# Experts' matrix products cut into four groups of 32 columns, and expert work dealt out step by step instead of in rounds of two steps

## What is computed

```python
# x: 2 batches x 2048 tokens x 256; H = 16 heads of 16; 8 experts, 256 -> 1024 -> 256
qk = (x @ Wqk).reshape(b, n, H, dh).transpose(0, 2, 1, 3)
v  = (x @ Wv ).reshape(b, n, H, dh).transpose(0, 2, 1, 3)
logits = (2.0 * qk @ qk.T - q2[..., :, None] - q2[..., None, :]) / math.sqrt(dh) * tau
out = softmax(logits) @ v                       # for each of 2 x 16 heads, 2048 x 2048
...
top1 = argmax(softmax(x @ router_W + router_b))  # one expert per token
h = relu(x @ W1[e] + b1[e])                      # 256 -> 1024
y = h @ W2[e] + b2[e]                            # 1024 -> 256
out = gate[e] * y
```

## Time and profile before

| what | value |
|---|---|
| median of 3 timed runs | 1456.67 us (1454.11 to 1459.45) |
| profiled execution, its own time | 1452.68 us |
| span of the profiled execution, first to last instruction | 1451.0 us |
| mean granted clock of TensorE | 0.993 of full speed |
| TensorE matmuls, busy | 1383.5 us, 95% |
| ScalarE, busy | 1066.9 us, 74% |
| VectorE, busy | 393.8 us, 27% |
| pairs 3 to 15, with expert work | 296.7 to 1329.0 us of the span |

### The profile page before, as it was taken

One profiled execution on the slowest core, in us unless ns is written; L12 is line 12 of the kernel. 1 busy time (PEld: TensorE's weight loads), 2 busy tenths in 40 slices (PEclk: granted clock), 3 DMA queues, 4 the chain that ended last, 5 costly groups with the idle time before them and its releaser, 6 DMA issues. The chain is left out here.

```text
span 1451.0 us, 26979 instructions
## 1 busy us (share of the span) xinstructions
PE 1383.5 (95%) x9041; PEld 659.9 (45%) x9041; DVE 393.8 (27%) x1009; ACT 1066.9 (74%) x1183; POOL 221.8 (15%) x310
## 2 busy tenths in 40 slices
PE   7999999999999999999999999999999999999978
PEld 5652222234444444444444444444444444445867
DVE  5863000012121211121121212111111212113977
ACT  5669999987777777777777777777777777774122
POOL 3111700001010010000010100100000101001860
PEclk9999999999999999999999999999999999999989
DMA  5779425526446444445464464443454645633423
GB/s 171 267 237 238 143 41 141 131 38 161 122 107 175 107 149 105 106 114 159 106 173 108 106 175 107 146 113 111 113 148 106 175 106 119 184 131 103 141 87 116
DMA packets 125520, 195.47 MB, mean 135 GB/s; under 512 B 22344, under 2 KB 91848, under 8 KB 122024
## 3 DMA queue, kind: packets, MB, share of 16 engines
q1 hardware_dynamic: 116440, 177.22, 44.6%
q0 software_dynamic: 9040, 17.71, 4.4%
HBM read 154.63 MB, written 35.95 MB: 131 GB/s over the span
## 5 line engine op out<-in xcount | busy, mean ns | idle before, releaser
L961 ACT ACTIVATE shared<-ps 128x1024 f32<-128x1024 f32 x1024 | 982.8, 1023 | 242.2 <-PE ps L1100 242.2
L1115 PE MATMUL ps<-shared,work 128*17 128x512 f32 x4096 | 502.5, 600 | 0.5 <-issue 0.5
L1100 PE MATMUL ps<-mov,stat 52*128 52x512 f32 x2048 | 420.6, 466 | 36.1 <-ACT shared L961 31.7
L1100 PEld LDWEIGHTS ps<-mov,stat 52*128 52x128 f32 x2048 | 168.6, 184 | 416.4 <-ACT shared L961 388.1
L1006 DVE TENSOR_SCALAR work<-ps,work 128x128 f32<-128x128 f32 x312 | 109.6, 351 | 590.3 <-PE ps L1167 575.4
L1115 PEld LDWEIGHTS ps<-shared,work 128*17 128x17 f32 x4096 | 89.7, 96 | 217.1 <-issue 203.6
L1167 PE MATMUL ps<-work,XNW 128*128 128x128 f32 x1248 | 180.7, 288 | 0.0
L1167 PEld LDWEIGHTS ps<-work,XNW 128*128 128x128 f32 x1248 | 151.0, 191 | 56.9 <-issue 56.9
L1151 PE MATMUL ps<-XNW,work 128*128 128x256 f32 x624 | 166.2, 382 | 0.0
L799 POOL DMA_DIRECT2D y_slots<-work x39 | 21.9, 563 | 760.1 <-DVE work L998 706.2
L1151 PEld LDWEIGHTS ps<-XNW,work 128*128 128x128 f32 x624 | 104.5, 191 | 11.4 <-issue 4.8
(11 more groups left out here) (168 smaller groups left out, 668.5 us busy)
## 6 DMA issues: line engine op xcount, KB each, us to landing
XNW<-in_L_ffn_W_dram SPq DMA_DIRECT2D x78, 1024.0 KB, 7.1
stat<-q_parts SPq DMA_DIRECT2D x192, 128.0 KB
mov<-q_parts SPq DMA_DIRECT2D x192, 64.0 KB
xg<-in_L_attn_x_dram SPq DMA_DIRECT2D x16, 512.0 KB, 4.7
q_parts<-XNW SPq DMA_DIRECT2D x16, 512.0 KB, 5.4
x_slots<-work SPq DMA_DIRECT2D x1, 4992.0 KB, 16.3
early<-x_slots SPq DMA_DIRECT2D x39, 128.0 KB, 2.1
early<-in_L_ffn_b_dram SPq DMA_DIRECT2D x39, 128.0 KB, 8.3
```

Of the source, the lines that this page charges most:

```text
L961: nc.scalar.activation(probs[:, s % DEEP, half * 1024:(half + 1) * 1024], ps[:, 2 * half:2 * half + 2].rearrange("p a b -> p (a b)"), ACT. ...
L1100: last = nc.tensor.matmul(ps[:, 2 * half + r], stat[rows, hh, m * P:(m + 1) * P], mov[rows, hh, half * 512:(half + 1) * 512], start=True, ...
L1115: last = nc.tensor.matmul(ps[32 * j:32 * j + VW, AV], Vh[:, hh, m], probs[:, s % DEEP, j * 512:(j + 1) * 512], start=(m == 0), stop=(m == ...
```

## The change

Every expert matmul is cut into four, each with 32 columns of weights and with `tile_position=(0, at)`, the form that `values` has. The transposes of `x` become matmuls with the identity in the same form. `expert_plan()` now makes 32 steps in place of 16 rounds: a tile takes 11 steps, `x` in the first, `h` of f in step 1+f, `y` of f in step 2+f. PE issues in each step: logits of the next step, the step's expert units (`y`, `x`, `h` in this order), `values` of this step. VectorE follows the same plan.

```diff
-        ROUNDS = STEPS // 2
+        CW = 32
...
-            rounds = [[] for _ in range(ROUNDS)]
+            steps = [[] for _ in range(STEPS)]
             for tt in range(3):
-                at = 5 * tt
-                rounds[at] += [("x", tt, 0), ("x", tt, 1)]
+                at = 11 * tt
+                steps[at] += [("x", tt, 0), ("x", tt, 1)]
                 for f in range(FC):
-                    rounds[at + 1 + f // 2].append(("h", tt, f))
-                    late = (f + 1) // 2 if tt < 2 else f // 2
-                    rounds[at + 2 + late].append(("y", tt, f))
-            return [sorted(r, key=lambda u: "xhy".index(u[0])) for r in rounds]
+                    steps[at + 1 + f].append(("h", tt, f))
+                    steps[at + 2 + f].append(("y", tt, f))
+            return [sorted(r, key=lambda u: "yxh".index(u[0])) for r in steps]
...
-                        ins = nc.tensor.matmul(ps[:, Y, 0:D], hT[:, b], w2s[:, a, b],
-                                               start=(b == 0), stop=(b == FC - 1))
+                        for at in range(0, P, CW):
+                            ins = nc.tensor.matmul(ps[at:at + CW, Y, 0:D], hT[:, b, at:at + CW], w2s[:, a, b],
+                                                   start=(b == 0), stop=(b == FC - 1), tile_position=(0, at))
...
-                        nc.tensor.transpose(ps[:, bank(k), 0:P], xs[:, a, b * P:(b + 1) * P],
-                                            ident[:, :]).then_inc(ring_ready, 1)
+                        for at in range(0, P, CW):
+                            last = nc.tensor.matmul(ps[at:at + CW, bank(k), 0:P], xs[:, a, b * P + at:b * P + at + CW],
+                                                    ident[:, :], start=True, stop=True, tile_position=(0, at))
+                        last.then_inc(ring_ready, 1)
...
                         for c in range(KC):
-                            last = nc.tensor.matmul(ps[:, bank(k), 0:P], w1s[:, a, c, b * P:(b + 1) * P],
-                                                    xsT[:, a, c], start=(c == 0), stop=(c == KC - 1))
+                            for at in range(0, P, CW):
+                                last = nc.tensor.matmul(ps[at:at + CW, bank(k), 0:P],
+                                                        w1s[:, a, c, b * P + at:b * P + at + CW], xsT[:, a, c],
+                                                        start=(c == 0), stop=(c == KC - 1), tile_position=(0, at))
...
-                    for n in range(ROUNDS):
-                        logits(i, 2 * n + 1)
-                        for u in rounds[n]:
-                            expert(i, u, use)
-                        if n + 1 < ROUNDS:
-                            logits(i, 2 * n + 2)
+                    for s in range(STEPS):
+                        if s + 1 < STEPS:
+                            logits(i, s + 1)
                         elif not last_one:
                             logits(i + 1, 0)
-                        values(i, 2 * n)
-                        values(i, 2 * n + 1)
+                        for u in steps[s]:
+                            expert(i, u, use)
+                        values(i, s)
```

More of the change, by code:

```diff
@@ L983, in expert_body @@
                 def expert_body(i):
-                    rounds = expert_plan()
-                    use = use_numbers(rounds)
-                    for n in range(ROUNDS):
-                        if n == 0:
+                    steps = expert_plan()
+                    use = use_numbers(steps)
+                    for s in range(STEPS):
+                        if s == 0:
                             turn_o(i - 1, 1)
-                        if n == ROUNDS // 2:
+                        if s == TB:
                             turn_o(i, 0)
-                        for u in rounds[n]:
+                        for u in steps[s]:
                             kind, a, b = u
```

## The result

The changed kernel takes 1461.29 us (median of 20 runs, 1455.89 to 1467.60) against 1456.91 us (20 runs) for the kernel before: ratio 1.0032, interval 1.0019 to 1.0044. That is 2.8 to 6.4 us slower. The forecast was slower by 10 us, 1467, with a range of 1430 to 1494. The profiled execution took 1467.6 us, the slowest of the 20, so its other stages have to be kept apart from the change.

What follows compares the result with a forecast made beforehand. PE was taken to bound full rounds, with PE and ACT waiting for each other in light ones. Pairs -22, jumps +24 and clock +8 us gave +10: 1463 profiled, 1467 on the timed runs' scale, range 1430 to 1494.

Steps and rivals of the forecast that it cites:

- The pair without the jump: Pairs 3 to 15: 77.5 us each in place of 79.18, -22 us over 13 pairs (-53 to +7).
- full step: Logits, h, y and values on PE, 21 steps a pair: 2.54 us each, against 5.12/2 = 2.56 before.
- light steps: The 11 steps a pair with x, h or y alone, or empty: 2.2 us taken as their mean.
- The bounds 1.98 and 2.4: Limits for a light step: 1.98 us as in pairs without experts, about 2.4 after a full step, when ACT starts late.
- The sets of four: Four 32-column matmuls side by side in the expert blocks on PE: 0.11 us a set for h, as one matmul before.
- rival 2: Expert sets of four on PE run slower than 0.11 us: +27 us, 1494 with the stall, 1462 without; chance 0.13.
- tail: Sets of four slower still: +187 us if each waits for its own loads, +200 at about 62 ns per matmul.
- The jumps: Ten jumps back of PE's loop over pairs 4 to 14 wait for code: 2.4 us exposed each, +24 us (+11 to +43).
- The 3.3 us: Wait for a code packet at a jump back, chosen nearer the quick 2.0 us transfer than the slow 8.3; bounds 2.0 and 5.2.
- the rest streams in behind its back: After a jump's first packet, later code arrives while PE works, a packet lasting 9 us of work: no further wait.
- The clock: Falls to half clock behind the jumps in every second pair, 1.66 us more each: +8 us (0 to +17).

Runs made afterwards that it cites:

- written-out form: The changed kernel with TensorE's hardware loop over pairs 4 to 14 replaced by eleven copies of its code: 1429.73 us, ratio 0.9816 to the kernel before.
- 1557: The changed kernel, looped, with x, y and the third tile's h back in the old whole form: 1489.86 us in one run against 1456.87 before.
- 2037: The changed kernel with its hardware loop, but the transposes of x back in the old whole form: ratio 1.0387 to the kernel before.
- 1749: The changed kernel with its hardware loop, but x and y back in the old whole form: ratio 1.0445 to the kernel before.
- the form alone: The kernel before, its 16 rounds kept, with four groups of 32 columns: 1508.35 us looped; ratio 0.9942 with pairs 4 to 14 written out.
- the plan alone: The kernel before with the new 32-step plan but the old whole matmuls and transposes: 1487.85 us, ratio 1.0210.

## Why the prediction came out as it did

**The pair without the jump** was right to the size: 77.5 us forecast, 77.52 measured in the written-out form, from 2.54 forecast and 2.53 measured per full step and a mean of 2.2 taken for light steps. Over 13 pairs -21.6 for the forecast -22. In the written-out form the starts of logits lie as follows in the first light steps of a pair:

```profile
531.25 0.73 PE L1099 MATMUL ps<-mov,stat 52*128 52x512 f32 x4
533.34 1.02 PE L1099 MATMUL ps<-mov,stat 52*128 52x512 f32 x4
535.73 0.73 PE L1099 MATMUL ps<-mov,stat 52*128 52x512 f32 x4
537.82 1.02 PE L1099 MATMUL ps<-mov,stat 52*128 52x512 f32 x4
540.64 0.73 PE L1099 MATMUL ps<-mov,stat 52*128 52x512 f32 x4
```

Steps of 2.09, 2.39 and 2.09 us, and then 2.82 for the first full one: what the light steps seem to save over 2.4, the next step pays in part. So the mean of 2.2 came out, in part because longer full steps behind light ones made up for shorter light steps. The bounds 1.98 and 2.4 held.

**The sets of four** run at 0.11 us, so rival 2 is out, with its tail.

**The jumps** came as forecast: 24 us forecast, 24.5 of idle PE measured, 2.45 each for 2.4. The 3.3 us behind that forecast was a choice between two far rows; the jump's instruction lasts 3.3 to 3.9 us in the trace, so the exact size owes something to luck. Shown by experiments: the wait goes with the jumps, appears in the old form when the body is long, and is gone when the body has 1557 instructions. The Trainium skill (Runtime: NRT & Kernel Launch, Instruction fetch mechanics) was right in the mechanism, a taken branch that waits for a fetch; its 2048 instructions would let the bodies of 2037 and 1749 stay, and these runs show that they do not. The body of 1557 touches 7 packets and that of 1749 touches 8; that one more is fetched ahead and all must share eight places would fit both, but no run shows the places themselves.

What the jumps cost in time is a little less than they idle. From the last `values` of a pair to the third `h` behind it PE needs 9.38 us in the written-out form. At the three jumps with neither a fall of the clock nor a large second wait it needs 11.65, 11.73 and 11.29, which is 2.2 more on the mean, 21.8 for ten jumps. Behind a jump the first logits block takes 0.66 us in place of 0.95, as its banks have long been read by then. The forecast put waits behind the jump at nothing ("the rest streams in behind its back"). At the jump of 784 us that was wrong: it needs 13.55 us, 2.0 more than a plain jump, because of the wait at 793.34.

**The clock** is the step that failed: "I take every second pair, +8 us" measured +5.6 us in the profiled execution and leaves about +2 in the timed ones. The mechanism was there: six falls in ten pairs, each behind a jump, where about five were forecast. A stretch at half clock right after the jump of 543.64 us:

```profile
543.90:547.30 3.40, 3.40 (x28) 0.99 (x26) 1.68 (x5) 1.94 (x2) 0.00 (x0) 0.50 0.90 331
```

The six jumps with a fall need 12.85 to 13.40 us for the same stretch, 1.5 more on the mean than plain ones, near the 1.66 that was forecast; six of them are 8.9 us. What was wrong is what this was compared with: the kernel before had two such falls in the stage, 3.3 us, and the sum against its own time never took them off. The clock's net part in this profile is 8.9 - 3.3 = +5.6 in place of +8.

The sum with measured terms is -21.6 + 21.8 + 2.0 + 5.6 = +7.8, against 7.7 in the stage of the two profiles. The medians say +4.4 (2.8 to 6.4). The rest, some 3 us, is again mostly the clock. The record has the mean granted clock of all 20 runs: 0.985 in the profiled one, 0.9875 at the median, and over the 20 a run with 0.001 less takes 1.5 us more. So 3.7 of the 6.3 us by which the profiled execution exceeds the median go with its lower clock; an estimate, as no other execution has a trace that shows where the falls lie. If the other terms are the same in the timed runs, the medians leave 4.4 - 2.2 = +2.2 us for the clock, against the +8 of the forecast.

So gain and loss of nearly equal size, 27 and 31 us by the ratios, leave a difference of 4 us. Errors of a few us in either move such a sum by its whole size: the forecast of +10 was an error of 5.6 us in terms that add up to 54.

## What to carry to other kernels

Count the instructions in the body of a hardware loop, weight loads and second passes of fp32 included, when a change multiplies them: here a body of 1557 stayed and one of 1749 did not. In the changed kernel every jump back left PE idle for 2.45 us and six of ten had a fall of the clock behind them, and writing the loop out cost nothing. A queue of instruction packets that is silent in later passes before a change and isn't after it is the sign to look for, along with idle time that ends with "issue". And where a work item in one form stands between items in two other forms, change form and order together: of the two halves of this change the form alone gained less (written out, 0.6 us a pair) and the plan alone lost.

## What the runs showed of the hardware

- A body of 1557 instructions stays on chip and one of 1749 does not: no packet of code against 74 of them in 540:1249.
- Instruction packets in order are free: 116 packets in the written-out kernel, no pair longer than 77.53 us.
- Waits for code away from the jump lie 256 instructions, or a multiple, apart: after 188, 1212, 16 and 49 instructions of four bodies that begin at three different places of the program.
- A jump target that is missing can be followed by a second wait, longer than the first (4.95 us behind 2.14), where the first edge of that grid lies only 16 instructions into the body.
- Four matmuls of 128 columns in four column groups, with 32 columns of weights each, run at 0.11 us a set, as one of 128 columns of weights does; between them and the product with V, which has the same form, no gap is seen.
